# Adaptive FFN with Strassen-type products: transposing the maxima of the next x at the end of a step and scaling it ahead of the routing

## The chip, the cores and the metric

The kernel runs on one core of one Trainium2 chip. The metric is the device time of one execution in microseconds (us), here the median of three runs. A core has TensorE (PE), VectorE (DVE), ScalarE (ACT), GpSimd (POOL) and SyncE (SP), each with its own instruction stream that is executed in order; they wait for each other through semaphores. All DMAs of this kernel are issued from SP.

## The reference

```python
w = weights[subjects]                                # 32 items, 128 x 128 each
y = einsum('bct,bcd->bdt', x, w)                     # x: 32 x 128 x 2048, f32
result = einsum('bnd,od->bno', y, W_base) + b_base   # W_base: 2048 x 2048
probs = softmax(einsum('bnd,ed->bne', y, W_gate))    # 8 experts
top_p, top_i = top_k(probs, 2); top_p /= sum(top_p)
route_w = sum(one_hot(top_i, 8) * top_p[..., None])
h = einsum('bnd,erd->bner', y, A)                    # rank 16 for each expert
delta = einsum('bner,eor->bno', h * route_w, B)
out = x + result + delta
```

## The kernel before, in words

Items go in pairs, 16 pairs. The contraction over 2048 is cut in two halves, so there are `NSTEP` = 32 steps: steps 0 to 15 (`n < NP`) do the first half of the contraction for each pair and store partial rows, steps 16 to 31 (`second`) do the second half, the routing and the low-rank `delta`. All matmuls are f16, each operand split in an upper and a lower part (three matmuls for one product, `three`). A step multiplies two blocks (`s` = 0 and 1) by a seven-product scheme: `product(n, s, q)`, q = 0 to 6, 12 matmuls of 128x512 each. Below, q0 to q6 are the products with s = 0.

While step n multiplies, step n+1 is prepared. The prepared x must be scaled by powers of two, and that takes a chain over four engines:

- `find_maxima` (DVE, lines 659 and 661) reduces the loaded x and the item weights to `amax`, 128x4.
- `transpose_maxima` (PE, line 1067) transposes `amax` into `bank_c`; `find_top` (DVE, lines 666, 652, 653, 670) makes the four maxima into a diagonal `top_diag`, 4x4, bf16.
- `spread_maxima` (PE, line 1071) spreads it over all partitions; `scale_x` (DVE, lines 675 to 679) makes `xw_scale` and sums half of x.
- `split_x_hi` (ACT, lines 466, 467) and `split_x_lo` (DVE, lines 684, 686) split x and the weights, twice each, and `cond(n+1, ...)` (PE, three matmuls a column, into `bank_c`) multiplies them. `cond(n+1, U_A11)` stands behind q5, needs the first `split_x_lo`, and is followed by q6.

The other work of a step: `make_features` (48 small matmuls into `bank_h`, between q0 and q1) gives the routing features; `features` (DVE, 728, 736) scales them. In the second half `route_tokens` (DVE, 745 to 767) computes the routing in small linked operations; its softmax needs one exponential from ACT (line 606 before, 610 in the change), which line 761 waits for. `weigh_features` (DVE, 774 to 788) gives `hw`, `transpose_hw` stands behind q4 on PE, ACT takes the upper part of the transposed `hwT` (line 611) and DVE the lower (794). `finish` (DVE, 716 and 720) joins products into output tiles: C11, C12, C21, C22 for each block; POOL adds each to the output rows (line 429; in the first half also the bias, line 419). `copy_p` (ACT, line 506) copies products from PSUM: P1 (q0), P5 (q1), U2 (q3) and P4 (q4). The U2 copy overwrites what C11 reads, so it waits for C11.

The order on each engine is the order in which the code is written; no scheduler changes it. Before step 0, PE, ACT, DVE and POOL prepare the first half of W (`w_quads`, `w_upper`, `w_sums_and_lower`, `w_lower`), and between steps 15 and 16 the second.

Of the kernel before, what the change touches and what calls it, by code (L numbers as in the profile page):

```python
# [13 lines left out]
NSTEP = 2 * NP  # L14
# [38 lines left out]
def adaln_ffn_kernel(nc, x, idx, w_cond, w_base, b_base, w_gate, a_lora, b_lora, out):  # L53
# [4 lines left out]
    with ExitStack() as ctx:  # L58
# [206 lines left out]
        P1_COPY, P5_COPY, U2_COPY, P4_COPY = range(4)  # L265
# [194 lines left out]
        def _(act):  # L460
            def split_x_hi(n, i):
                if i == 0:
                    act.wait_ge(x_scaled, n + 1)
                else:
                    act.wait_ge(xs_added, n + 1)
                nc.scalar.activation(XP[:, 0, i, :], X[:, i, :], ACT.Copy, scale=xw_scale[:, i:i + 1])
                nc.scalar.activation(WCP[:, 0, i, :], WC[:, i, :], ACT.Copy,
                                     scale=xw_scale[:, 2 + i:3 + i]).then_inc(xp_hi, 1)
# [24 lines left out]
            def copy_p(n, s, i):  # L493
                par = n % 2
                src, q, at, row = ((BX[s], 0, 0, 0), (BY[1], 1, 1, 1), (BX[s], 3, 0, 0), (BZ, 4, 2, 1))[i]
                act.wait_ge(prod_done, n_prod(n, s, q))
                before = 2 * n + s - 1
                if i == P1_COPY and before >= 0:
                    act.wait_ge(t_done, n_tile(before // 2, before % 2, C12))
                elif i == U2_COPY:  # L500
                    act.wait_ge(t_done, n_tile(n, s, C11))
                elif i == P5_COPY and before >= 0:
                    act.wait_ge(t_done, n_tile(before // 2, before % 2, C22))
                elif i == P4_COPY and before >= 0:
                    act.wait_ge(t_done, n_tile(before // 2, before % 2, C21))
                nc.scalar.activation(PC[:, at, :], src[:, :], ACT.Copy,  # L506
                                     scale=y_inv[:, par, row:row + 1]).then_inc(p_copied, 1)
# [93 lines left out]
            for n in range(NSTEP):  # L601
                more = n + 1 < NSTEP
                copy_p(n, 0, P1_COPY)
                if n >= NP:
                    act.wait_ge(shifted_ready, n - NP + 1)
                    nc.scalar.activation(exps[:, :, :], shifted[:, :, :], ACT.Exp).then_inc(exps_ready, 1)
                copy_p(n, 0, P5_COPY)
                copy_p(n, 0, U2_COPY)
                if n >= NP:
                    act.wait_ge(hwT_filled, n - NP + 1)  # L610
                    nc.scalar.activation(hwT[:, 0, :], BD[:, 0:2 * P], ACT.Copy).then_inc(hwT_hi, 1)
                if more:
                    split_x_hi(n + 1, 0)
                    split_x_hi(n + 1, 1)
                copy_p(n, 0, P4_COPY)
                if more:
                    copy_a(n + 1, U_A11)
                    s_upper(n + 1, A11)
                    copy_a(n + 1, U_S1)
                    s_upper(n + 1, S1)  # L620
                copy_p(n, 1, P1_COPY)
                if more:
                    copy_a(n + 1, U_A12)
                    s_upper(n + 1, A12)
                    s_upper(n + 1, S2)
                copy_p(n, 1, P5_COPY)
                if more:
                    copy_a(n + 1, U_A22)
                    s_upper(n + 1, A22)
                    s_upper(n + 1, S4)  # L630
                    s_upper(n + 1, S3)
                copy_p(n, 1, U2_COPY)
                copy_p(n, 1, P4_COPY)
                if n == NP - 1:
                    sum_rows(NU)
                    for g in range(NU, 2 * NU):
                        if g + 1 < 2 * NU:
                            sum_rows(g + 1)
                        w_upper(g)
                    act.wait_ge(w_sum_lo, 4 * 2 * NU)  # L640

        @block.vector
        def _(dve):
# [283 lines left out]
            w_sums_and_lower(7)  # L927

            find_maxima(1)
            for n in range(NSTEP):  # L930
                more, second = n + 1 < NSTEP, n >= NP
                features(n)
                if more:
                    find_top(n + 1)
                if second:
                    route_tokens(n)
                    weigh_features(n)
                finish(n, 0, C11)
                if more:
                    scale_x(n + 1)  # L940
                if second:
                    split_hwT_lo(n)
                if more:
                    split_x_lo(n + 1, 0)
                    split_x_lo(n + 1, 1)
                finish(n, 0, C12)
                if second:
                    add_delta(n, 0)
                finish(n, 0, C21)
                finish(n, 0, C22)  # L950
                if second:
                    add_delta(n, 1)
                if more:
                    s_lower(n + 1, A11)
                    s_lower(n + 1, S1)
                if second:
                    add_delta(n, 2)
                if more:
                    sum_s2(n + 1)
                    s_lower(n + 1, A12)  # L960
                if second:
                    add_delta(n, 3)
                finish(n, 1, C11)
                if more:
                    s_lower(n + 1, S2)
                if second:
                    add_delta(n, 4)
                if more:
                    sum_s4_s3(n + 1)
                    s_lower(n + 1, A22)  # L970
                if second:
                    add_delta(n, 5)
                if more:
                    s_lower(n + 1, S4)
                    s_lower(n + 1, S3)
                if n + 2 < NSTEP:
                    find_maxima(n + 2)
                finish(n, 1, C12)
                if second:
                    add_delta(n, 6)  # L980
                    add_delta(n, 7)
                finish(n, 1, C21)
                finish(n, 1, C22)
                if n == NP - 1:
                    dve.wait_ge(r_added, 8 * NP)
                    w_scales(NU)
                    for g in range(NU, 2 * NU):
                        if g + 1 < 2 * NU:
                            w_scales(g + 1)
                        w_sums_and_lower(g)  # L990

        @block.tensor
        def _(pe):
# [158 lines left out]
            cond(0, U_A22)  # L1152
            w_quads(6)
            w_quads(7)

            for n in range(NSTEP):
                more, second = n + 1 < NSTEP, n >= NP
                if n in (0, NP):
                    prepared = NU * (1 + n // NP)
                    pe.wait_ge(w_lo, 3 * prepared)  # L1160
                    pe.wait_ge(w_sum_lo, 4 * prepared)
                    pe.wait_ge(w_inv, prepared)
                product(n, 0, 0)
                make_features(n)
                if more:
                    transpose_maxima(n + 1)
                for q in range(1, NPROD):
                    product(n, 0, q)
                    if q == 2 and more:
                        spread_maxima(n + 1)  # L1170
                    if q == 4 and second:
                        transpose_hw(n)
                    if q == 5 and more:
                        cond(n + 1, U_A11)
                    if q == 6:
                        if more:
                            cond(n + 1, U_S1)
                        if second:
                            delta(n, 0)
                for q in range(NPROD):  # L1180
                    product(n, 1, q)
                    if q < 2 and more:
                        cond(n + 1, (U_A12, U_A22)[q])
                    if second and q < 6:
                        delta(n, q + 1)
                        if q == 5:
                            delta(n, 7)
                if n == NP - 1:
                    pe.wait_ge(p_copied, n_copy(n, 1, P4_COPY))
                    pe.wait_ge(t_done, n_tile(n, 1, C22))  # L1190
                    pe.wait_ge(h_ready, NP)
                    for g in range(NU, 2 * NU):
                        pe.wait_ge(stage_in[2 * g % 4], 16 * (g // 2 + 1))
                        pe.wait_ge(stage_in[(2 * g + 1) % 4], 16 * (g // 2 + 1))
                        w_quads(g)
# [27 lines left out]
```

## Time and profile before

| What | Value |
|---|---|
| Median of 3 runs | 1655.74 us (1655.5 to 1656.36) |
| The profiled execution | 1655.53 us, its span 1653.7 us |
| PE busy | 1530.8 us (93%) |
| DVE busy | 1301.4 us (79%) |
| ACT busy | 595.5 us (36%) |
| POOL busy | 615.8 us (37%) |
| Granted TensorE clock, mean | 0.973 |

Busy time of an engine is the sum of its instructions' spans. In the timeline of this trace a matmul of 128x512 is shown 0.38 us long, though the next one starts some 0.215 us after it: the ends are modelled. So PE times are best taken from start to start.

### The profile page before, as it was taken

To read this page: it belongs to the slowest core of one execution; us is meant where nothing else is said; L and a number is where in the kernel's file an instruction comes from. 1 tells how busy PE (TensorE), PEld (TensorE's weight loads), DVE (VectorE), ACT (ScalarE), POOL (GpSimd) and SP (SyncE) were. 2 spreads that over 40 slices of the span, in tenths; PEclk is the share of its full clock that TensorE was granted. 3 is DMA by queue.
4 is the path that set the end of the run, shared out by engine and by line. 5 is a ranking of instruction groups with operands and counts; after the bars stand their busy time and mean duration, and the time that the engine had idled before them with its cause. 6 is when DMAs were issued, how large, how long until landed. Compare 5 with 4: busy or idle time off the path is not lost.

```text
span 1653.7 us, 25726 instructions
## 1 busy us (share of the span) xinstructions
PE 1530.8 (93%) x9539; PEld 832.7 (50%) x9539; DVE 1301.4 (79%) x2234; ACT 595.5 (36%) x996; POOL 615.8 (37%) x467
## 2 busy tenths in 40 slices
PE   5359999999999999999659999999999999999998
PEld 4245555555555555555454555545554554554553
DVE  4777888888888888888776888888888888888874
ACT  6563333333333333333583322333332233333231
POOL 2253555555555555555461212212221221221222
PEclk9679999999999999999889999999999999999999
DMA  5243444444444444444622334434324443332432
GB/s 193 87 143 90 134 134 134 135 135 132 134 133 132 128 135 134 135 135 137 212 89 79 93 99 134 133 98 129 111 82 121 134 119 111 122 102 84 135 106 70
DMA packets 102911, 201.87 MB, mean 122 GB/s; under 512 B 10874, under 2 KB 24186, under 8 KB 102266
## 3 DMA queue, kind: packets, MB, share of 16 engines
q1 hardware_dynamic: 102786, 200.22, 39.4%
q8 instruction: 76, 1.25, 0.3%
q14 instruction: 49, 0.40, 0.1%
HBM read 128.96 MB, written 71.22 MB: 121 GB/s over the span
## 4 chain that ended last, share of the span: by engine, by line
PE 76%; DVE 15%; ACT 4%; issue 4%; DMA 1%; POOL 1%; SPq 0%; POOLq 0%; ACTq 0%; DVEq 0%
PE bank_x L995 9%; PE bank_x L996 9%; PE bank_x L997 9%; PE bank_y L997 8%; PE bank_y L996 8%; PE bank_y L995 8%; PE bank_h L997 3%; PE bank_h L995 3%; PE bank_h L996 3%; PE bank_z L997 3%; PE bank_z L995 3%; PE bank_z L996 3%; PE bank_c L995 2%; PE bank_c L996 2%; PE bank_c L997 2%
## 5 line engine op out<-in xcount | busy, mean ns | idle before, releaser
L429 POOL TENSOR_TENSOR x_res<-x_res,t_sums 128x512 f32<-128x512 f32 x256 | 344.7, 1349 | 924.6 <-DVE t_sums L720 769.7
L995 PE MATMUL bank_x<-TT,s_parts 128*128 128x512 f16 x768 | 293.1, 382 | 13.3 <-POOL TT L413 7.5
L996 PE MATMUL bank_x<-TT,s_parts 128*128 128x512 f16 x768 | 292.8, 381 | 0.0
L997 PE MATMUL bank_x<-TT,s_parts 128*128 128x512 f16 x768 | 292.6, 381 | 0.0
L995 PE MATMUL bank_y<-TT,s_parts 128*128 128x512 f16 x768 | 291.1, 379 | 0.0
L996 PE MATMUL bank_y<-TT,s_parts 128*128 128x512 f16 x768 | 291.1, 379 | 0.0
L997 PE MATMUL bank_y<-TT,s_parts 128*128 128x512 f16 x768 | 291.1, 379 | 0.0
L506 ACT ACTIVATE p_copies<-bank_x,y_inv 128x512 f32<-128x512 f32 x128 | 87.4, 683 | 440.5 <-PE bank_x L997 346.6
L491 ACT ACTIVATE s_parts<-a_full 128x512 f16<-128x512 f32 x224 | 141.0, 630 | 270.6 <-DVE a_full L698 123.3
L720 DVE TENSOR_TENSOR t_sums<-t_sums,inv_w 128x512 f32<-128x512 f32 x256 | 218.7, 854 | 8.8
L419 POOL TENSOR_TENSOR x_res<-x_res,BT 128x512 f32<-128x512 f32 x128 | 199.3, 1557 | 1.2
L693 DVE TENSOR_TENSOR s_parts<-a_full,s_parts 128x512 f16<-128x512 f32 x224 | 192.0, 885 | 3.0 <-ACT s_parts L491 3.0
L716 DVE SCALAR_TENSOR_TENSOR t_sums<-bank_y,y_inv,p_copies 128x512 f32<-128x512 f32 x128 | 95.3, 745 | 78.2 <-PE bank_y L997 77.3
L995 PEld LDWEIGHTS bank_x<-TT,s_parts 128*128 128x128 f16 x768 | 75.3, 98 | 96.2 <-issue 15.3
L997 PEld LDWEIGHTS bank_x<-TT,s_parts 128*128 128x128 f16 x768 | 75.5, 98 | 91.8 <-issue 1.9
L997 PEld LDWEIGHTS bank_y<-TT,s_parts 128*128 128x128 f16 x768 | 75.2, 98 | 90.6
L716 DVE SCALAR_TENSOR_TENSOR t_sums<-bank_x,y_inv,p_copies 128x512 f32<-128x512 f32 x128 | 95.2, 744 | 30.7 <-PE bank_x L997 30.7
L996 PEld LDWEIGHTS bank_x<-TT,s_parts 128*128 128x128 f16 x768 | 75.4, 98 | 82.0 <-issue 1.4
L996 PEld LDWEIGHTS bank_y<-TT,s_parts 128*128 128x128 f16 x768 | 75.1, 98 | 81.7
L995 PEld LDWEIGHTS bank_y<-TT,s_parts 128*128 128x128 f16 x768 | 75.2, 98 | 81.2
L995 PE MATMUL bank_c<-w_cond_parts,x_parts 128*128 128x128 f16 x512 | 93.0, 220 | 23.7 <-DVE w_cond_parts L686 15.5
L474 ACT ACTIVATE a_full<-bank_c 128x512 f32<-128x512 f32 x128 | 76.1, 594 | 101.2 <-PE bank_c L997 101.2
(214 smaller groups left out, 2717.6 us busy)
## 6 DMA issues: line engine op xcount, KB each, us to landing
x<-in_x_dram SPq DMA_DIRECT2D x32, 1024.0 KB, 5.5
x_res<-in_x_dram SPq DMA_DIRECT2D x128, 256.0 KB, 3.7
part_scratch<-x_res SPq DMA_DIRECT2D x128, 256.0 KB, 3.0
x_res<-part_scratch SPq DMA_DIRECT2D x128, 256.0 KB, 4.0
out_dram<-x_res SPq DMA_DIRECT2D x128, 256.0 KB, 3.0
x_res<-in_L_ffn_W_base_dram SPq DMA_DIRECT2D x12, 512.0 KB, 4.6
w_cond<-in_L_cond_weights_dram SPq DMA_DIRECT2D x64, 64.0 KB, 3.9
a_full<-in_L_ffn_W_base_dram SPq DMA_DIRECT2D x8, 512.0 KB, 4.7
```

The lines of the kernel that those rows point to most:

```text
L419: link(nc.gpsimd.tensor_tensor(XR[:, xr_slot(m), :], XR[:, xr_slot(m), :], bias[:, o:o + Q], ALU.add))
L429: nc.gpsimd.tensor_tensor(XR[:, xr_slot(m), :], XR[:, xr_slot(m), :], TM[:, m % 2, :], ALU.add).then_inc(r_added, 1)
L474: nc.scalar.activation(AF[:, u, :], BC[:, :], ACT.Copy, scale=Y_DOWN).then_inc(af_copied, 1)
L491: nc.scalar.activation(SO[:, slot(n, q), 0, :, :], quads(AF[:, af_of[q], :]), ACT.Copy).then_inc(s_hi, 1)
L506: nc.scalar.activation(PC[:, at, :], src[:, :], ACT.Copy, scale=y_inv[:, par, row:row + 1]).then_inc(p_copied, 1)
L693: nc.vector.tensor_tensor(SO[:, slot(n, q), 1, :, :], quads(AF[:, af_of[q], :]), SO[:, slot(n, q), 0, :, :], ALU.subtract).then_inc(s_lo, 1)
L716: nc.vector.scalar_tensor_tensor(out=TM[:, m % 2, :], in0=src[:, :], scalar=y_inv[:, n % 2, c // 2:c // 2 + 1], in1=PC[:, at, :], op0=ALU. ...
L720: nc.vector.tensor_tensor(TM[:, m % 2, :], TM[:, m % 2, :], inv_w[:, o:o + Q], ALU.mult).then_inc(r_ready, 1)
L995: nc.tensor.matmul(dst, lhs[0], rhs[0], start=start, stop=False, skip_group_check=chained)
L996: nc.tensor.matmul(dst, lhs[0], rhs[1], start=False, stop=False, skip_group_check=chained)
L997: return nc.tensor.matmul(dst, lhs[1], rhs[0], start=False, stop=stop, skip_group_check=chained)
```

## The change

`transpose_maxima(n + 2)` now stands at the end of step n on PE, behind the last product, and the one for step 1 in front of step 0. `spread_maxima(n + 1)` stands right behind `make_features(n)`, where it was between q2 and q3. On DVE, `find_top(n + 2)` stands at the end of step n, and `scale_x(n + 1)` right behind `features(n)`, in front of the routing and of C11. On ACT the P5 copy and both `split_x_hi` stand in front of the exponential. The number of instructions on each engine is the same, and on SP and POOL nothing moves.

```diff
@@ ScalarE, the loop over the steps
                 copy_p(n, 0, P1_COPY)
+                copy_p(n, 0, P5_COPY)
+                if more:
+                    split_x_hi(n + 1, 0)
+                    split_x_hi(n + 1, 1)
                 if n >= NP:
                     act.wait_ge(shifted_ready, n - NP + 1)
                     nc.scalar.activation(exps[:, :, :], shifted[:, :, :], ACT.Exp).then_inc(exps_ready, 1)
-                copy_p(n, 0, P5_COPY)
                 copy_p(n, 0, U2_COPY)
                 if n >= NP:
                     act.wait_ge(hwT_filled, n - NP + 1)
                     nc.scalar.activation(hwT[:, 0, :], BD[:, 0:2 * P], ACT.Copy).then_inc(hwT_hi, 1)
-                if more:
-                    split_x_hi(n + 1, 0)
-                    split_x_hi(n + 1, 1)
                 copy_p(n, 0, P4_COPY)
@@ VectorE
             find_maxima(1)
+            find_top(1)
             for n in range(NSTEP):
                 more, second = n + 1 < NSTEP, n >= NP
                 features(n)
                 if more:
-                    find_top(n + 1)
+                    scale_x(n + 1)
                 if second:
                     route_tokens(n)
                     weigh_features(n)
                 finish(n, 0, C11)
-                if more:
-                    scale_x(n + 1)
                 if second:
                     split_hwT_lo(n)
@@
                 finish(n, 1, C21)
                 finish(n, 1, C22)
+                if n + 2 < NSTEP:
+                    find_top(n + 2)
@@ TensorE
             w_quads(7)
+            transpose_maxima(1)
@@
                 make_features(n)
                 if more:
-                    transpose_maxima(n + 1)
+                    spread_maxima(n + 1)
                 for q in range(1, NPROD):
                     product(n, 0, q)
-                    if q == 2 and more:
-                        spread_maxima(n + 1)
@@
                         if q == 5:
                             delta(n, 7)
+                if n + 2 < NSTEP:
+                    transpose_maxima(n + 2)
```

TensorE in front of step 0, before. The matmuls of line 1021 are the last of the preparation of W, the first of line 995 belongs to `product(0, 0, 0)`:

```order
L1004 MATMUL bank_h<-diag_inv,ones 128x128 x2
L1021 MATMUL bank_y<-diag,BT 128x128 x4
L1021 MATMUL bank_z<-diag,x_res 128x128 x4
L1021 MATMUL bank_x<-diag,BT 128x128 x4
L1021 MATMUL bank_x<-diag,x_res 128x128 x4
L995 MATMUL bank_x<-TT,s_parts 128x512
```

The same place in the change (its lines are one higher here):

```order
L1005 MATMUL bank_h<-diag_inv,ones 128x128 x2
L1022 MATMUL bank_y<-diag,BT 128x128 x4
L1022 MATMUL bank_z<-diag,x_res 128x128 x4
L1022 MATMUL bank_x<-diag,BT 128x128 x4
L1022 MATMUL bank_x<-diag,x_res 128x128 x4
L1068 MATMUL bank_c<-ident,amax 4x128
L996 MATMUL bank_x<-TT,s_parts 128x512
```

The transpose of the maxima of step 1 now stands in front of the first product.

ScalarE in a step of the second half, from the P1 copy, before (`p_copies` from `bank_x` is P1 and then U2, from `bank_y` P5, from `bank_z` P4):

```order
L506 ACTIVATE p_copies<-bank_x,y_inv 128x512
L606 ACTIVATE exps<-shifted 128x16
L506 ACTIVATE p_copies<-bank_y,y_inv 128x512
L506 ACTIVATE p_copies<-bank_x,y_inv 128x512
L611 ACTIVATE hwT<-bank_d 128x256
L466 ACTIVATE x_parts<-x,xw_scale 128x1024
L467 ACTIVATE w_cond_parts<-w_cond,xw_scale 128x128
L466 ACTIVATE x_parts<-x,xw_scale 128x1024
L467 ACTIVATE w_cond_parts<-w_cond,xw_scale 128x128
L506 ACTIVATE p_copies<-bank_z,y_inv 128x512
```

The same place in the change:

```order
L506 ACTIVATE p_copies<-bank_x,y_inv 128x512
L506 ACTIVATE p_copies<-bank_y,y_inv 128x512
L466 ACTIVATE x_parts<-x,xw_scale 128x1024
L467 ACTIVATE w_cond_parts<-w_cond,xw_scale 128x128
L466 ACTIVATE x_parts<-x,xw_scale 128x1024
L467 ACTIVATE w_cond_parts<-w_cond,xw_scale 128x128
L610 ACTIVATE exps<-shifted 128x16
L506 ACTIVATE p_copies<-bank_x,y_inv 128x512
L614 ACTIVATE hwT<-bank_d 128x256
L506 ACTIVATE p_copies<-bank_z,y_inv 128x512
```

The exponential moved behind the P5 copy and the four operations that split x.

VectorE from the end of one step of the second half into the next, the difference:

```order
+L666 TENSOR_REDUCE amax_top<-bank_c 4x1
+L652 TENSOR_SCALAR top_clamped<-amax_top 4x1
+L653 TENSOR_SCALAR top_pow<-top_clamped 4x1
+L670 TENSOR_SCALAR top_diag<-ident,top_pow 4x4
 L728 SCALAR_TENSOR_TENSOR h<-bank_h,y_inv,inv_ag 128x136 x2
 L736 TENSOR_TENSOR h<-h,h_first 128x272
-L666 TENSOR_REDUCE amax_top<-bank_c 4x1
-L652 TENSOR_SCALAR top_clamped<-amax_top 4x1
-L653 TENSOR_SCALAR top_pow<-top_clamped 4x1
-L670 TENSOR_SCALAR top_diag<-ident,top_pow 4x4
+L675 COPY pow<-bank_c 128x4
+L676 RECIPROCAL rpow<-pow 128x4
```

The four operations of `find_top` moved in front of the features, right behind C22 of the step before, and `scale_x` follows the features.

## Rows read from the trace of the kernel before

**Rows 1.** Timeline in front of step 0: start us, us, engine, line, op, out<-in, shapes, xcount

```profile
119.00 0.59 PE L995 MATMUL bank_x<-TT,s_parts 128*128 128x512 f16 x1 [7.45 <-POOL TT L413]
...
121.66 2.29 DVE L659 TENSOR_REDUCE amax<-x 128x2 f32<-128x2048 f32 x1 [4.52 <-DMA x<-in_x_dram]
123.86 0.41 DVE L661 TENSOR_REDUCE amax<-w_cond 128x2 f32<-128x256 f32 x1
```

**Rows 2.** Timeline of TensorE, step 23 (second half); in brackets idle us and its releaser

```profile
1217.07 0.27 PE L1067 MATMUL bank_c<-ident,amax 128*4 128x128 f32 x1
1217.18 0.38 PE L995 MATMUL bank_y<-TT,s_parts 128*128 128x512 f16 x1
...
1222.14 0.38 PE L997 MATMUL bank_y<-TT,s_parts 128*128 128x512 f16 x1
1222.45 0.17 PE L1071 MATMUL bank_c<-top_diag,ones 4*128 4x4 bf16 x1
1222.56 0.39 PE L995 MATMUL bank_x<-TT,s_parts 128*128 128x512 f16 x1
...
1231.74 0.23 PE L995 MATMUL bank_c<-w_cond_parts,x_parts 128*128 128x128 f16 x1 [1.02 <-DVE w_cond_parts L686]
```

**Rows 3.** Timeline of VectorE, end of step 22 and step 23

```profile
1214.92 1.27 DVE L720 TENSOR_TENSOR t_sums<-t_sums,inv_w 128x512 f32<-128x512 f32 x1
...
1218.41 0.28 DVE L666 TENSOR_REDUCE amax_top<-bank_c 4x1 f32<-4x128 f32 x1
...
1219.07 0.22 DVE L670 TENSOR_SCALAR top_diag<-ident,top_pow 4x4 bf16<-4x4 f32 x1
...
1221.68 0.17 DVE L761 TENSOR_REDUCE exp_sum<-exps 128x2 f32<-128x16 f32 x1
...
1225.37 0.42 DVE L788 SCALAR_TENSOR_TENSOR hw<-hw,hw_rpow 128x256 f32<-128x256 f32 x1
...
1226.49 0.69 DVE L720 TENSOR_TENSOR t_sums<-t_sums,inv_w 128x512 f32<-128x512 f32 x1
...
1230.13 1.28 DVE L684 SCALAR_TENSOR_TENSOR x_parts<-x,xw_scale,x_parts 128x1024 f16<-128x1024 f32 x1 [0.39 <-ACT w_cond_parts L467]
1231.34 0.35 DVE L686 SCALAR_TENSOR_TENSOR w_cond_parts<-w_cond,xw_scale,w_cond_parts 128x128 f16<-128x128 f32 x1
```

**Rows 4.** Timeline of GpSimd: adding C21 and C22 of step 22, C11 of step 23

```profile
1214.37 1.27 POOL L429 TENSOR_TENSOR x_res<-x_res,t_sums 128x512 f32<-128x512 f32 x1 [1.44 <-DVE t_sums L720]
1216.34 1.27 POOL L429 TENSOR_TENSOR x_res<-x_res,t_sums 128x512 f32<-128x512 f32 x1 [0.69 <-DVE t_sums L720]
1227.33 1.27 POOL L429 TENSOR_TENSOR x_res<-x_res,t_sums 128x512 f32<-128x512 f32 x1 [9.73 <-DVE t_sums L720]
```

**Rows 5.** Timeline of the preparation of W: `find_top(0)` beside GpSimd

```profile
71.03 1.17 DVE L670 TENSOR_SCALAR top_diag<-ident,top_pow 4x4 bf16<-4x4 f32 x1
...
71.03 1.15 POOL L413 TENSOR_TENSOR TT<-t_sums,TT 128x512 f16<-128x512 f32 x1
```

**Rows 6.** Timeline of ScalarE, step 23

```profile
1219.60 0.22 ACT L606 ACTIVATE exps<-shifted 128x16 f32<-128x16 f32 x1 [4.49 <-DVE shifted L746]
1219.97 0.69 ACT L506 ACTIVATE p_copies<-bank_y,y_inv 128x512 f32<-128x512 f32 x1
...
1226.55 0.69 ACT L506 ACTIVATE p_copies<-bank_x,y_inv 128x512 f32<-128x512 f32 x1 [5.89 <-DVE t_sums L716]
1228.17 0.38 ACT L611 ACTIVATE hwT<-bank_d 128x256 f16<-128x256 f32 x1 [0.93 <-PE bank_d L1095]
1228.66 1.15 ACT L466 ACTIVATE x_parts<-x,xw_scale 128x1024 f16<-128x1024 f32 x1
```

**Rows 7.** Timeline of VectorE, GpSimd and TensorE where a first-half step begins

```profile
251.84 0.99 DVE L720 TENSOR_TENSOR t_sums<-t_sums,inv_w 128x512 f32<-128x512 f32 x1
...
252.35 1.60 POOL L429 TENSOR_TENSOR x_res<-x_res,t_sums 128x512 f32<-128x512 f32 x1
...
253.63 0.27 PE L1067 MATMUL bank_c<-ident,amax 128*4 128x128 f32 x1
```

## The prediction

> **What bounds the kernel now.** I first read the page: TensorE is busy 93% of the span at a mean clock of 0.973, so it sets the pace, and what counts is where it idles. Then the list of waits of TensorE, then the timeline of one step of each half, all engines side by side. In the steps of the first half TensorE runs product after product and never waits. In steps 16 to 30 it waits once a step: cond(n+1, U_A11), behind q5, starts at 1231.74 after 1.02 us of idleness, released by split_x_lo on VectorE [rows 2, 3]. Because the modelled end of the matmul ahead of it lies 0.17 us past the point at which a next one could start (0.38 shown, 0.215 from start to start), the whole loss is 1.19 us a step, 15 times. That is all the change can win: 17.9 us.
>
> What VectorE did in that time is a chain: features, find_top, routing, hw, C11, scale_x, then the split on ScalarE and VectorE. The change takes find_top and scale_x off its end. So I follow the new chain, with TensorE's first matmul of q1 (1217.18 before) as its zero. Before, cond starts 14.56 us after it [rows 2].
>
> **The start.** PE runs in order, and transpose_maxima(1) now stands in front of the first product. It needs find_maxima(1), whose x lands late: VectorE waited 4.52 us for that DMA and ended line 661 at 124.27. TensorE had begun step 0 at 119.00 [rows 1]. In the change its first product can start at 124.27, plus 0.05 for the semaphore (line 686 ends at 1231.69, cond starts at 1231.74 [rows 2, 3]), plus 0.11 for the transpose: 124.4, **5.4 us later**. Before, a whole product of the step covered this reduction. Nothing behind it has slack for it, since the first half is TensorE's. The shown 0.59 us of the matmul at 119.00, against 0.38 in step 23, says that TensorE restarts at its lower clock after the idle time [rows 1, 2]; it does so after a longer idle time too, so I add nothing, and bound the term by 3 and 8 us.
>
> **The transpose and the spread, as such.** The transpose costs 0.11 us on TensorE (1217.07 to 1217.18) wherever it stands. The spread between q2 and q3 cost 0.21: the last matmul of q2 starts at 1222.14, the spread at 1222.45, q3 at 1222.56, 0.42 where 0.21 is usual [rows 2]. Behind the features it costs 0.11 as long as it needn't wait.
>
> **It will wait.** top_diag is made by the last operation of find_top, line 670, now directly behind C22. In step 22, C22's line 720 ends at 1216.19, line 670 would start 0.58 later (line 666 starts 0.08 before the end of its predecessor, line 670 0.66 after line 666) at 1216.77. But GpSimd's add of C22 runs from 1216.34 to 1217.61 [rows 3, 4]. Do the two disturb each other? The one time that line 670 met a GpSimd add, it took 1.17 us instead of 0.22 and ended 0.02 us after that add [rows 3, 5]. Hence it ends at 1217.63, and the spread starts at 1217.68. TensorE comes to it at 1217.18 (1217.07, and 0.11 later because the transpose is now in front of q0): it idles 0.50 us. q1 starts at 1217.79 instead of 1217.18, **+0.61 a step**, against TensorE's other work; 0.21 of it is saved again at q3.
>
> In the first half: line 720 ends at 252.83, line 670 would start at 253.41, GpSimd's add lasts to 253.95, so line 670 ends at 253.97, the spread starts at 254.02, q1 at 254.13. Before it started 0.11 behind the transpose, at 253.74 [rows 7]. +0.39, less the 0.21 saved: **+0.18 a step**, for steps 1 to 15 (find_top(1) and find_top(17) have time enough): 2.7 us. The rest of a first-half step stays under TensorE's cover: the splits now come earlier, and cond did not wait before. If line 670 were not held, the spread wouldn't wait: 0.11 less 0.21, -0.10 a step.
>
> **The new chain of a second-half step**, from the start of q1. The P5 copy follows the end of q1: 1219.97 less 1217.18, at 2.79 [rows 2, 6]. It blocks ScalarE some 0.6 (0.69 shown, the next starts 0.1 earlier). The scale has long been there, so both split_x_hi follow: one pair takes from 1228.66 to just before 1230.13, 1.43, two with their overlaps 2.7 [rows 3, 6]. Only then comes the exponential, 0.22 [rows 6]: VectorE can start line 761 at 6.31 (2.79 + 0.58 + 2.68 + 0.22 + 0.04). Is it VectorE that is late? From the end of line 670 at 1217.63 it has the features (1.2, from the end of TensorE's features some 0.15 after 1217.07 to line 666 at 1218.41), scale_x (at most 2.6: from 1227.18 to 1230.13 less 0.39 idle, and it met an add of GpSimd's there) and the routing up to line 761 (2.39, from 1219.29 to 1221.68) [rows 3]. It is ready at 1223.8 or sooner, 6.0 after q1 at most: ScalarE decides, and VectorE waits for the exponential, which before was there in time. Behind the exponential everything is queued on VectorE: line 788 starts 3.69 later, C11 behind it.
>
> From line 761: hw at 3.69; the U2 copy, which waits for C11, at 4.87 (1226.55 less 1225.37); hwT on ScalarE at 5.45, its end at 5.83; the lower part of hwT on VectorE (shaped as line 788, 0.42) from 5.87; split_x_lo could start at 6.20. GpSimd's add of C11 starts at 5.65 (1227.33 less 1225.37, plus 3.69) and ends at 6.92 [rows 3, 4, 6]. Line 684 reads two tensors in SBUF, as line 720 does, and line 720 took 1.27 us instead of 0.69 when the add of C21 at 1214.37 had begun before it, going on about 0.14 before that add's end at 1215.64 [rows 3, 4]. So line 684 is taken up at 6.78, and cond starts 1.61 after it (1231.74 less 1230.13), at 8.39. With 6.31 that is 14.70 after q1.
>
> That line 684 itself is held is in no row: it never met an add before, and took 1.28 us, as in step 23. The page "SBUF — State Buffer" of the Trainium skill, section "Who interferes with whom", says that a VectorE instruction with two SBUF inputs contends with a GpSimd instruction that reads SBUF and that the later one is blocked to the end. By that rule cond starts at 14.70; were the page wrong for this instruction, 14.12. The trace agrees for line 720, 1.27 against 0.69 [rows 3].
>
> A step of the second half changes by 14.70 - 14.56 = +0.14 in the chain and +0.61 in the start of q1: **+0.75 us**, for steps 17 to 30, 10.5 us; step 16 has only the +0.14. transpose_hw waits 0.1 or so on the way (line 788 ends 4.11 after 761, at 10.4; TensorE is there at 10.3), which is hidden in front of cond. So the wait for split_x_lo does not go: it stands behind the exponential instead of behind scale_x.
>
> **Sum.** 5.4 + 2.7 + 0.1 + 10.5 = 18.7. The profiled execution took 1655.53 us (span 1653.7, and 1.8 around it), the median is 0.2 above it: 1674.4 us.
>
> **Rivals.**
> - *The splits are not held by GpSimd's add.* Then the chain is 8.39 less 0.58 long, cond at 14.12: 0.44 less in step 16, +0.17 in 14 steps. 5.4 + 2.7 - 0.4 + 2.4 = 10.1: 1665.8 us. For it: that no row shows line 684 held; against it: line 720. Chance 0.15.
> - *Line 670 is not held at the end of a step.* q1 starts 0.5 sooner in the second half and 0.28 in the first. 5.4 - 1.5 + 0.1 + 14 x 0.25 = 7.5: 1663.2 us. Against it stands the one case that there is [rows 5]. Chance 0.08. Both together: 5.4 - 1.5 - 0.4 - 14 x 0.33 = -1.1, 1654.6 us, within what can be told from no change; chance 0.04.
> - *Faster: the exponential is not on the path, cond finds its input ready.* Then a step has +0.40 at q3 and -1.19 at cond: 14 times -0.79, step 16 -1.4, with 5.4 + 2.7: -4.4, 1651.4 us. For it: x's split now stands early on ScalarE. Its point: cond could start 13.2 after q1 (14.56 less 1.19 and 0.21), so the exponential would have to come 1.5 us sooner than 6.31. It would without the two splits in front of it. Chance 0.07.
> - *More than that:* the idle time at the start costs more clock, or the collisions with GpSimd, whose adds now meet more of VectorE's work, spread on: 1680 us, chance 0.08.
> - The forecast itself has 0.58.
>
> **How the numbers follow.** The range goes from under the first two rivals (1662) to 1679; outside are the rivals below and part of the last. A measurement of this kernel tells some 0.2%, 3.3 us, from no change. Faster by more than that: 0.07. Within it: 0.05. Slower: 0.88.
>
> **What the profile of the changed kernel would show.** Step 0's first matmul at some 124.4. Line 670 with about 0.55 us in the first half and 0.86 in the second. TensorE waiting for top_diag at the spread, 0.3 us in 15 steps and 0.5 in 14. VectorE idle in front of line 761 for the exponential, 0.3 us or more. The lower split's first operation near 1.9 us in the second half, and TensorE still waiting for line 686 in 15 steps, 1.0 us and more by the modelled ends. A second-half step 0.75 us longer than before, a first-half step 0.18. I am wrong if line 761 finds the exponential ready, or if the first product of step 0 starts as before.

## The result, and the profile after

| What | Before | Changed |
|---|---|---|
| Median of 5 runs | 1655.74 us (1654.92 to 1656.44) | 1674.44 us (1672.8 to 1674.85) |
| Ratio | | 1.0111, 95% interval 1.0098 to 1.0123 |
| The profiled execution | 1655.53 us, span 1653.7 | 1674.5 us, span 1672.7 |

The change costs 18.7 us. The page of the changed kernel, its part on busy time:

```profile
PE 1537.3 (92%) x9539; PEld 834.4 (50%) x9539; DVE 1324.4 (79%) x2234; ACT 592.5 (35%) x996; POOL 630.4 (38%) x467
```

The work of TensorE is the same and its share is smaller: the time went into waits. VectorE and GpSimd are busy 23 and 15 us longer with the same number of instructions: an operation that one of them is made to wait in by the other (it is *held*) shows as a longer one. On VectorE line 684 is busy 23.3 us longer in all, line 686 15.8 and line 670 14.4. Line 677 (`xw_scale`, 128x4) is busy 27.1 us less: before, it was held too, in 31 of 32 steps. In step 23:

```profile
1227.50 1.12 DVE L677 TENSOR_SCALAR xw_scale<-rpow 128x4 f32<-128x4 f32 x1
```

before, ending 0.02 us after GpSimd's add of C11 [rows 4], and in the change:

```profile
1232.55 0.17 DVE L677 TENSOR_SCALAR xw_scale<-rpow 128x4 f32<-128x4 f32 x1
```

The split of x on ScalarE started 0.04 us after the held one ended [rows 6], so this hold was part of the chain that made cond late before. No kernel removes it alone.

The list of waits, TensorE's and the one of VectorE that matters (who waited, for whom, us in total, times, longest us):

```profile
PE bank_c L996 <- DVE w_cond_parts L686: 16.7, 15, 1.1
PE bank_c L1072 <- DVE top_diag L670: 14.6, 15, 9.9
PE bank_c L1068 <- DVE amax L661: 12.5, 1, 12.5
...
DVE exp_sum L761 <- ACT exps L610: 26.3, 15, 2.1
```

The wait for the lower split (line 686) that the change might have removed is still there, 15 times. Two are new: TensorE for `top_diag` (9.9 of the 14.6 us is one wait in the preparation, which the kernel before has too; the other 14 are 0.34 us each, in the second half), and once for the maxima. VectorE's wait for the exponential is new too.

The timeline of VectorE, GpSimd, ScalarE and TensorE where step 23 begins; it answers to [rows 2 to 4] and [rows 6]. The columns are as there:

```profile
1230.26 0.85 DVE L670 TENSOR_SCALAR top_diag<-ident,top_pow 4x4 bf16<-4x4 f32 x1
...
1237.62 0.17 DVE L761 TENSOR_REDUCE exp_sum<-exps 128x2 f32<-128x16 f32 x1 [1.75 <-ACT exps L610]
...
1243.49 0.42 DVE L794 SCALAR_TENSOR_TENSOR hwT<-bank_d,hwT 128x256 f16<-128x256 f32 x1 [0.36 <-ACT hwT L614]
1243.83 1.78 DVE L684 SCALAR_TENSOR_TENSOR x_parts<-x,xw_scale,x_parts 128x1024 f16<-128x1024 f32 x1
```

```profile
1229.82 1.26 POOL L429 TENSOR_TENSOR x_res<-x_res,t_sums 128x512 f32<-128x512 f32 x1 [0.70 <-DVE t_sums L720]
1243.27 1.26 POOL L429 TENSOR_TENSOR x_res<-x_res,t_sums 128x512 f32<-128x512 f32 x1 [12.18 <-DVE t_sums L720]
```

```profile
1234.07 0.69 ACT L506 ACTIVATE p_copies<-bank_y,y_inv 128x512 f32<-128x512 f32 x1 [5.36 <-PE bank_y L998]
1234.65 1.14 ACT L466 ACTIVATE x_parts<-x,xw_scale 128x1024 f16<-128x1024 f32 x1
...
1237.32 0.20 ACT L610 ACTIVATE exps<-shifted 128x16 f32<-128x16 f32 x1
```

```profile
1231.16 0.17 PE L1072 MATMUL bank_c<-top_diag,ones 4*128 4x4 bf16 x1 [0.34 <-DVE top_diag L670]
1231.27 0.39 PE L996 MATMUL bank_y<-TT,s_parts 128*128 128x512 f16 x1
...
1245.93 0.23 PE L996 MATMUL bank_c<-w_cond_parts,x_parts 128*128 128x128 f16 x1 [1.12 <-DVE w_cond_parts L686]
```

Read from above: line 670 begins 0.44 us after GpSimd's add and ends 0.03 us after it. 0.05 us later TensorE spreads, and q1 starts at 1231.27. The exponential starts 6.05 us after q1, behind P5 and both splits; VectorE had stood 1.75 us before it came. GpSimd's add of C11 begins at 1243.27; the first lower split comes up at 1243.83, takes 1.78 us and ends 1.08 us after that add. cond starts 14.66 us after q1, against 14.56 before.

The timeline in front of step 0 and at a first-half step, as [rows 1] and [rows 7]:

```profile
121.12 2.29 DVE L659 TENSOR_REDUCE amax<-x 128x2 f32<-128x2048 f32 x1 [4.23 <-DMA x<-in_x_dram]
123.33 0.41 DVE L661 TENSOR_REDUCE amax<-w_cond 128x2 f32<-128x256 f32 x1
...
257.79 0.56 DVE L670 TENSOR_SCALAR top_diag<-ident,top_pow 4x4 bf16<-4x4 f32 x1
```

```profile
256.74 1.59 POOL L429 TENSOR_TENSOR x_res<-x_res,t_sums 128x512 f32<-128x512 f32 x1
```

```profile
123.79 0.37 PE L1068 MATMUL bank_c<-ident,amax 128*4 128x128 f32 x1 [12.50 <-DVE amax L661]
124.00 0.59 PE L996 MATMUL bank_x<-TT,s_parts 128*128 128x512 f16 x1
...
258.41 0.17 PE L1072 MATMUL bank_c<-top_diag,ones 4*128 4x4 bf16 x1
```

The first product starts at 124.00, 5.0 us later than in [rows 1], because the transpose in front of it waits for an x that lands late. In the first-half step line 670 ends 0.02 us after GpSimd's add, and the spread follows it by 0.06.

To see where the 19 us of span (1672.7 against 1653.7) went, take the first matmul of `make_features` in steps 1, 15, 16 and 31; from one step's to the next one's is a period. Timeline of the changed kernel:

```profile
170.69 0.22 PE L996 MATMUL bank_h<-FT,s_parts 128*128 128x136 f16 x1
...
762.79 0.22 PE L996 MATMUL bank_h<-FT,s_parts 128*128 128x136 f16 x1
...
881.68 0.32 PE L996 MATMUL bank_h<-FT,s_parts 128*128 128x136 f16 x1
...
1622.91 0.22 PE L996 MATMUL bank_h<-FT,s_parts 128*128 128x136 f16 x1
```

and of the kernel before:

```profile
166.59 0.22 PE L995 MATMUL bank_h<-FT,s_parts 128*128 128x136 f16 x1
...
755.99 0.22 PE L995 MATMUL bank_h<-FT,s_parts 128*128 128x136 f16 x1
...
873.36 0.22 PE L995 MATMUL bank_h<-FT,s_parts 128*128 128x136 f16 x1
...
1603.93 0.22 PE L995 MATMUL bank_h<-FT,s_parts 128*128 128x136 f16 x1
```

| Stretch | Before | Changed | More | Forecast |
|---|---|---|---|---|
| Up to step 1 | 166.59 | 170.69 | 4.10 | 5.4 |
| Steps 1 to 15, 14 periods | 589.40 | 592.10 | 2.70 (0.19 each) | 2.5 |
| Step 15 to 16, with the second half of W | 117.37 | 118.89 | 1.52 | 0.2 |
| Steps 16 to 31, 15 periods | 730.57 | 741.23 | 10.66 | 10.6 |

### The profile page after: what moved, and what is told of

It is laid out like the page before. It is cut to its first block, busy times and chain, and to the rows that moved or that the text cites. A ratio compares the mean times of both kernels' runs of the same rounds, so it can differ in the third digit from the quotient of the medians.

```text
span 1672.7 us, 25710 instructions
## 1 busy us (share of the span) xinstructions
PE 1537.3 (92%) x9539; PEld 834.4 (50%) x9539; DVE 1324.4 (79%) x2234; ACT 592.5 (35%) x996; POOL 630.4 (38%) x467
## 4 chain that ended last, share of the span: by engine, by line
PE 62%; DVE 23%; ACT 7%; issue 5%; DMA 1%; POOL 0%; SPq 0%; DVEq 0%; POOLq 0%; ACTq 0%
PE bank_y L996 8%; PE bank_x L996 8%; PE bank_x L998 8%; PE bank_x L997 8%; PE bank_y L998 8%; PE bank_y L997 8%; DVE t_sums L716 3%; DVE amax L659 2%; DVE t_sums L720 2%; ACT x_parts L466 2%; PE bank_c L996 2%; PE bank_z L998 2%; PE bank_z L996 2%; PE bank_z L997 2%; PE bank_c L998 2%
## 5 line engine op out<-in xcount | busy, mean ns | idle before, releaser
L429 POOL TENSOR_TENSOR x_res<-x_res,t_sums 128x512 f32<-128x512 f32 x256 | 359.1, 1405 | 928.7 <-DVE t_sums L720 773.7
```

Source lines behind the costliest of these rows:

```text
L429: nc.gpsimd.tensor_tensor(XR[:, xr_slot(m), :], XR[:, xr_slot(m), :], TM[:, m % 2, :], ALU.add).then_inc(r_added, 1)
```

## The experiments

All ran beside the kernel before, whose median in the three series was 1655.42, 1655.33 and 1655.53 us. The change is at 1674.44, from the series in which the kernel before had 1655.74. A timeline is that of one execution. The executions of one kernel lie 1.2 to 2.8 us apart, so medians that differ by less than some 1.5 us are not told apart here.

**Step 0 in the old order.** In step 0 alone TensorE and VectorE keep the order of before:

```diff
             w_quads(7)
-            transpose_maxima(1)
...
                 make_features(n)
-                if more:
+                if n == 0:
+                    transpose_maxima(1)
+                elif more:
                     spread_maxima(n + 1)
                 for q in range(1, NPROD):
                     product(n, 0, q)
+                    if q == 2 and n == 0:
+                        spread_maxima(1)
...
                 features(n)
-                if more:
+                if n == 0:
+                    find_top(1)
+                elif more:
                     scale_x(n + 1)
```

(and `scale_x(1)` behind C11, `find_top(1)` no longer in front of the loop).

> The changed kernel, with step 0 alone in the order of before: transpose_maxima(1) behind make_features(0), its spread behind q2, find_top(1) and scale_x(1) at their old places on VectorE. Steps 1 to 31 as in the change. Theory (TensorE's first product stands behind the transpose and so behind the late x): the first product starts near 119 again and the whole comes 4 to 5 us sooner than the change, some 1670 us. Rival (the late start is absorbed later, or the clock takes it back): within 1 us of 1674.4.

Measured: 1667.64 us (1667.31 to 1668.64), ratio 1.0075 (1.0061 to 1.0088), 6.8 us under the change. The first product starts at 118.69 and `make_features` of step 1 at 165.83, 4.9 us sooner than in the change, and that stays to step 15. A further 1.4 us falls between steps 15 and 16 and 0.6 behind step 16, where both programs are the same; more on that below. The theory holds, the rival falls.

**The exponential first.** ScalarE in the order P1, exponential, P5, splits; all else as in the change:

```diff
                 copy_p(n, 0, P1_COPY)
+                if n >= NP:
+                    act.wait_ge(shifted_ready, n - NP + 1)
+                    nc.scalar.activation(exps[:, :, :], shifted[:, :, :], ACT.Exp).then_inc(exps_ready, 1)
                 copy_p(n, 0, P5_COPY)
                 if more:
                     split_x_hi(n + 1, 0)
                     split_x_hi(n + 1, 1)
-                if n >= NP:
-                    act.wait_ge(shifted_ready, n - NP + 1)
-                    nc.scalar.activation(exps[:, :, :], shifted[:, :, :], ACT.Exp).then_inc(exps_ready, 1)
```

> The changed kernel, with the exponential on ScalarE back in front of the P5 copy and of the splits of x. Theory (the exponential behind P5 and four split operations is what makes VectorE's chain late): line 761 no longer waits 1.75 us for the exponential, it starts some 4.6 us after q1 instead of 6.35, and cond comes at 13.1 to 13.3 after q1 instead of 14.66, practically without a wait: 15 x 1.4 to 1.5, 1652 to 1654 us. Rival (another link holds cond, such as hwT on ScalarE or GpSimd's add before the split): the wait shrinks by less than half, 1664 us or more.

Measured: 1651.66 us (1650.42 to 1652.43), ratio 0.9976 (0.9967 to 0.9986): 22.8 us under the change, and under the kernel before. Its timeline where step 23 begins, VectorE, GpSimd and TensorE:

```profile
1224.36 0.17 DVE L761 TENSOR_REDUCE exp_sum<-exps 128x2 f32<-128x16 f32 x1
...
1230.93 0.42 DVE L794 SCALAR_TENSOR_TENSOR hwT<-bank_d,hwT 128x256 f16<-128x256 f32 x1 [1.07 <-ACT hwT L614]
1231.27 1.28 DVE L684 SCALAR_TENSOR_TENSOR x_parts<-x,xw_scale,x_parts 128x1024 f16<-128x1024 f32 x1
```

```profile
1230.00 1.27 POOL L429 TENSOR_TENSOR x_res<-x_res,t_sums 128x512 f32<-128x512 f32 x1 [10.46 <-DVE t_sums L720]
```

```profile
1219.62 0.17 PE L1072 MATMUL bank_c<-top_diag,ones 4*128 4x4 bf16 x1 [0.34 <-DVE top_diag L670]
1219.72 0.39 PE L996 MATMUL bank_y<-TT,s_parts 128*128 128x512 f16 x1
...
1232.90 0.22 PE L996 MATMUL bank_c<-w_cond_parts,x_parts 128*128 128x128 f16 x1
```

Line 761 starts 4.64 us after q1 with no idle time in brackets, cond 13.18 after q1 and without a wait. The split now comes up as GpSimd's add ends, so it is not held either: 1.28 us. So the 1.48 us that cond gains on q1 have two parts: the collision, which the lateness caused and which is worth 0.5 by the kernel further down that removes it alone, and the lateness itself.

**The exponential behind P5.** As above, but with P5 left in front of it:

```diff
                 copy_p(n, 0, P1_COPY)
                 copy_p(n, 0, P5_COPY)
+                if n >= NP:
+                    act.wait_ge(shifted_ready, n - NP + 1)
+                    nc.scalar.activation(exps[:, :, :], shifted[:, :, :], ACT.Exp).then_inc(exps_ready, 1)
                 if more:
                     split_x_hi(n + 1, 0)
                     split_x_hi(n + 1, 1)
```

(the exponential behind the splits goes).

> The changed kernel with the exponential between the P5 copy and the splits of x. Of what stands in front of it in the change only the splits (2.7 us) go, the P5 copy (from the end of q1 on) stays. The exponential would come some 3.4 us after q1, VectorE is ready for it at 4.6: nothing is lost against having it first, 1651 to 1652.5 us. Rival (P5, which waits for q1, is a good part of the delay): 1656 us or more.

Measured: 1650.78 us (1649.98 to 1651.71), ratio 0.9972 (0.9962 to 0.9983). The exponential starts 3.38 us after q1, and line 761 at 4.64 as above. P5 in front of the exponential costs nothing; the four split operations cost it all.

**The diagonal by ScalarE.** `find_top(n)` ends with `top_pow2` for n > 0, and ScalarE, idle at the end of a step, makes `top_diag`:

```diff
+            def make_diag(n):
+                act.wait_ge(top_ready, n)
+                act.wait_ge(amax_spread, n)
+                nc.scalar.activation(top_diag[:, :], ident[0:4, 0:4], ACT.Copy,
+                                     scale=top_pow2[:, 0:1]).then_inc(amax_top_ready, 1)
...
                 copy_p(n, 1, U2_COPY)
                 copy_p(n, 1, P4_COPY)
+                if n + 2 < NSTEP:
+                    make_diag(n + 2)
```

> The changed kernel, with top_diag of steps 1 to 31 made by ScalarE instead of VectorE's line 670, at the same place in the program; same values. Theory (line 670 is held by GpSimd's add of C22 and holds the spread): ScalarE is not held, the spread no longer waits, 0.28 us less in each of 15 first-half steps and 0.5 in each of 14 second-half steps: 11 us, 1663 us. Rival (the spread is late because find_top as such comes too late behind C22, and the 1.2 GHz hand-over costs as much): 1671 us or more.

Measured: 1665.68 us (1664.4 to 1667.05), ratio 1.006 (1.0047 to 1.0074), 8.8 us under the change. TensorE's timeline at a spread of the second half has no idle time any more, and the hand-over through ScalarE is in time:

```profile
1225.36 0.22 PE L1013 MATMUL bank_h<-FT,s_parts 128*128 128x136 f16 x1
1225.51 0.17 PE L1087 MATMUL bank_c<-top_diag,ones 4*128 4x4 bf16 x1
1225.62 0.39 PE L1011 MATMUL bank_y<-TT,s_parts 128*128 128x512 f16 x1
```

```profile
1225.01 0.30 ACT L465 ACTIVATE top_diag<-ident,top_pow 4x4 bf16<-4x4 f32 x1 [9.74 <-DVE top_pow L681]
```

A first-half period is back at 42.10 us (42.29 in the change, 42.10 before), a second-half one goes from 49.40 to 49.00. So the hold of line 670 is shown as the cause of the wait at the spread. I had expected 11 us, from 0.28 and 0.5 us a step; the steps gained 0.19 and 0.4. The rows say why: from the last matmul of the features to q1 it is 0.26 us even without a wait, where 0.06 is the usual distance of those matmuls. The spread behind the features costs 0.20 us, about the 0.21 that it cost between q2 and q3, and not 0.11. The kernel with neither transpose nor spread behind the features (the last one below) says the same: from the first matmul of the features to q1 it takes 2.84 us, here 3.04.

**GpSimd's add of C11 behind the split.**

```diff
+                if n >= NP and j == 0 and n + 1 < NSTEP:
+                    pool.wait_ge(xp_lo, 2 * (n + 1) + 1)
                 pool.wait_ge(r_ready, m + 1)
```

> The changed kernel, with GpSimd's add of C11 in steps 16 to 30 waiting for the first lower split of x. Theory (line 684 is held by that add): line 684 takes 1.28 instead of 1.78 us, cond comes 0.5 us sooner in 15 steps, 7.5 us, 1667 us. Rival (line 684 is slow for another reason, or the add that comes later holds what follows): 1672 us or more.

Measured: 1665.71 us (1665.09 to 1667.05), ratio 1.0061 (1.0048 to 1.0075), 8.7 us under the change. VectorE's split and GpSimd's add in step 23:

```profile
1240.14 1.27 DVE L686 SCALAR_TENSOR_TENSOR x_parts<-x,xw_scale,x_parts 128x1024 f16<-128x1024 f32 x1
...
1241.59 1.28 DVE L686 SCALAR_TENSOR_TENSOR x_parts<-x,xw_scale,x_parts 128x1024 f16<-128x1024 f32 x1
```

```profile
1241.81 2.19 POOL L431 TENSOR_TENSOR x_res<-x_res,t_sums 128x512 f32<-128x512 f32 x1 [14.41 <-DVE w_cond_parts L688]
```

The split takes 1.27 instead of 1.78 us, and now it is the add that is held by the second split, 2.19 instead of 1.26, which costs TensorE nothing that shows. The period of a second-half step is 48.89 instead of 49.40. cond still waits, but starts 14.15 us after q1 (1227.58) instead of 14.66:

```profile
1241.73 0.23 PE L998 MATMUL bank_c<-w_cond_parts,x_parts 128*128 128x128 f16 x1 [0.60 <-DVE w_cond_parts L688]
```

**Both holds away, the exponential still late.** The last two edits together.

> The changed kernel with both meetings with GpSimd removed (top_diag by ScalarE, GpSimd's add of C11 behind the first lower split), the exponential left behind the splits. If the two holds are separate costs, 8.8 and 8.7 us come off: 1656 to 1658 us, so that what is left over the kernel before is the late x at the start. Rival (they overlap, since both act on the same chain): 1661 us or more.

Measured: 1658.81 us (1657.65 to 1660.21), ratio 1.0019 (1.001 to 1.0029), 15.6 us under the change where the two alone gave 8.8 and 8.7; I had expected 1656 to 1658. In the steps they add: a first-half step takes 42.10 us and a second-half step 48.48, 0.92 less than in the change where the two alone gave 0.40 and 0.51. In the profiled execution (the slowest of 11, 1660.21 us) step 1 comes 5.8 us later than before and the stretch between steps 15 and 16 takes 2.2 us more; the steps of the second half are 0.21 us each under those of the kernel before. So the 3.3 us over the kernel before are the start and the middle, less what the second half saves.

**Putting the useful parts together.** Four more kernels look for what of the change is worth having. The first joins the old order of step 0 and the early exponential:

> Both mendings together: the exponential back in front of the P5 copy, and step 0 in the order of before. The two costs lie in different steps, so they should add: 22.8 and some 5 to 6.8 us under the change, 1645 to 1647 us. Rival (one hides part of the other): 1650 us.

Measured: 1645.64 us (1644.87 to 1646.24), ratio 0.994 (0.9926 to 0.9954), 28.8 us under the change where the two alone gave 6.8 and 22.8. They nearly add.

The next has `make_diag` as well:

> As c1, and top_diag of steps 1 to 31 by ScalarE, so that nothing behind C22 is held by GpSimd. If the hold of line 670 is a cost of its own, 15 x 0.2 and 14 x 0.5 us come off again: 1636 to 1638 us, and TensorE waits neither at the spread nor at cond. Rival (with the exponential early, GpSimd's add of C11 becomes the bound of cond, since it starts with VectorE's chain): only the first half gains, 1643 us.

Measured: 1638.92 us (1638.26 to 1639.47), ratio 0.9901 (0.9886 to 0.9916). TensorE's waits for line 686 and for `top_diag` in the loop are both gone; this version is faster than the kernel before by 1.0% and than the change by 2.1%. That is 1 us over the 1636 to 1638 expected: a second-half step takes 47.55 us against 47.90, and the stretch between steps 15 and 16 took 118.51 us in the profiled execution against 117.64 in the version without `make_diag`.

The third keeps the change's step 0 and has x of step 1 loaded sooner:

```diff
             sp.wait_ge(w_tr, 4 * (NU - 1))
+            sp.wait_ge(xp_lo, 2)
+            load_x(1)
             for m in range(4):
                 load_tile(m)
```

> The changed kernel with the exponential first and top_diag by ScalarE, step 0 as in the change, but SyncE issues the load of step 1's x in front of the first tiles of x_res and the bias. If the late x alone is what held the first product, it starts within 1.5 us of 119 with the transpose still in front of it: within 2 us of c2. Rival (the transfers of W and the bias then come late instead): 2 us or more above c2.

Measured: 1641.23 us (1640.38 to 1642.12), ratio 0.9916 (0.9902 to 0.9929). The first product starts at 119.73, though the transpose is still in front of it: the late x alone made it late. The total is 2.3 us above the version with the old step 0, which is where I had put the rival (2 us or more). The steps do not differ (42.10 us, and 47.54 against 47.55). Of the 2.1 us between the two profiled executions, 0.4 is the later start (119.29 there), 1.0 the product q0 of step 0 (5.01 us at a granted clock of 0.51, 4.00 at 0.64 there) and 0.9 the stretch between steps 15 and 16. Whether the earlier load has a part in the last two is not shown.

The last takes one part of the change only, the transpose and `find_top` at the end of a step, with the spread, `scale_x` and ScalarE as before:

```diff
                 finish(n, 1, C21)
                 finish(n, 1, C22)
+                if n + 2 < NSTEP:
+                    find_top(n + 2)
```

> The kernel of before with one part of the change: the maxima are transposed and find_top done at the end of a step (in step 0 at their old places). The spread stays behind q2, scale_x behind C11, ScalarE as before. Theory: find_top's 0.8 us leave VectorE's chain in front of the routing, of which the hold of line 670 gives back 0.3; TensorE meets no wait at the spread, cond comes 0.5 us sooner in 15 steps, 7 to 8 us, 1648 us. Rival (GpSimd's add of C11 or of C22 takes it back, as in the change): 1654 us or more.

Measured: 1651.62 us (1651.18 to 1652.85), ratio 0.9978 (0.9969 to 0.9987), a gain of 3.7 us, half of what I expected. The timeline of ScalarE in step 23 says why:

```profile
1226.40 0.39 ACT L611 ACTIVATE hwT<-bank_d 128x256 f16<-128x256 f32 x1 [1.46 <-PE bank_d L1097]
1226.68 1.14 ACT L466 ACTIVATE x_parts<-x,xw_scale 128x1024 f16<-128x1024 f32 x1
```

VectorE's chain is 0.5 us shorter (line 761 starts 3.98 us after q1 against 4.50, rows 2 and 3), but the splits stand on ScalarE behind the upper part of hwT, and that waits for a transpose behind q4 on TensorE, 10.99 us after q1 as before. So the split starts at 11.27 against 11.48, and a second-half step takes 48.47 us against 48.69: ScalarE's queue took 0.3 of the 0.5 us.

## Why the prediction was right

Its forecast, 1674.4 us, was met at 1674.44, and the sum is right in its two large places for the reasons given. That it fits to 0.1 us is luck: terms missed in opposite ways, and the start and the middle differ by more than that from one execution to the next.

- **The start, 5.4 us forecast.** The mechanism holds, with the old step 0 and with the early x. The first product started 5.0 us late, x having landed 0.5 us sooner in this execution; by step 1 it was 4.1. TensorE's product q0 took 4.59 us at a granted clock of 0.56, before 5.07 at 0.50 (the lower level, 1.2 GHz, all through). In this execution the term was 1.3 us too large. In the profiled executions of the five other kernels with the late x in front of the first product, step 1 began 4.35 to 5.76 us later than before, so 5.4 was a fair size and 4.1 a low draw.
- **The spread waits, 0.18 a step in the first half.** 0.19 measured. Line 670 took 0.56 us there and 0.85 in the second half, where 0.55 and 0.86 were forecast. The rival that line 670 is not held falls. But the prediction priced the spread behind the features at 0.11 us where it costs 0.20, and so counted a step without the wait 0.10 under the kernel before; with the diagonal made by ScalarE it is level with it, 42.10 us. As long as the spread waits, this error drops out of the sum, because the wait ends when line 670 does; it makes the rivals in which line 670 is not held too fast, by 0.1 us a step.
- **The chain of a second-half step, 14.70 after q1.** 14.66 measured, and q1 0.61 later as forecast: 0.71 a step (10.66 in all) where 0.75 in 14 steps and 0.14 in one were forecast. That one, step 16, took 0.68 more and not 0.14: some 0.35 is the lower clock, at which its features began (3.40 us from their first matmul to q1, 3.05 in the kernel with the old step 0), and 0.2 the transpose at its end and the dearer spread, which the sum left out there. Each link is in the profile: P5 at 2.80, the exponential at 6.05, line 761 at 6.35, cond 8.31 behind it. VectorE was ready for the exponential at 4.60, well before the 6.0 that the prediction gave as its bound.
- **The exponential decides.** Shown by both kernels that move it. The rival in which cond finds its input ready was put to the test: it is what the kernel becomes when the splits stand behind the exponential, with cond 13.18 after q1, the 13.2 given as its point, and a step 0.79 us under the one before (47.90 against 48.69), the -0.79 given.
- **The split is held by GpSimd's add.** This was in no row of before and rested on line 720's example and on the page "SBUF — State Buffer" of the Trainium skill, section "Who interferes with whom", whose rule on two SBUF inputs was weighed there. By that rule, the trace agrees: 1.78 us instead of 1.28, and 1.27 when the add stays away, with cond at 14.15 where the prediction had 14.12 for a split that is not held. Its sign "near 1.9 us" was 0.1 too large, with the split ending 1.08 us after the add.
- **A sign that came out smaller.** TensorE's waits for `top_diag` show in the 14 steps of the second half alone, at 0.34 us; 0.3 in 15 steps and 0.5 in 14 were forecast. The ends of matmuls are modelled, so this list shows less than the start of q1 does, which came as late as forecast.
- **What the sum did not have.** 1.5 us between steps 15 and 16, where 0.2 was forecast. The changed kernel's q0 of step 16 took 5.07 us at a granted clock of 0.50, before 4.21 at 0.61 (from its first matmul to the features), which is 0.9 of it. Six kernels, the change among them, have the same program in this stretch. Two took 118.9 us (the change, and the one with the later add of C11; q0 at 0.50 in both), four 117.1 to 117.6 (the exponential first, behind P5, the old step 0, and the two mendings together; q0 at 0.63 to 0.65), and the kernel before 117.4. So it is not caused by an instruction that the change moves there, and as each kernel has one profile it may be no more than the difference between two executions; what tips it was not tested.

The forecast "1654.6, within no change" for the case that neither hold occurs can be set beside the kernel that removes both, 1658.81: 4.2 us off. The steps explain some 3 of them, 0.10 in each of the first half (42.10, not 42.00) and 0.12 in each of the second (0.21 under the kernel before, not 0.33), most of it the price of the spread; the rest lies in the start and the middle.

## What to carry to other kernels

An operation moved to the front of an in-order queue is paid for by what it overtakes: here four idle-looking operations on an engine that is busy 36% delayed one exponential of 0.2 us, on which 4 us of another engine's work and the very input they were to hurry were waiting. Before you move a link of a chain, list what else passes through each queue it goes to, and check what the other user of a shared resource does at the new time; small operations fit an idle gap only if nobody holds them in it. A preload hoisted in front of a loop needs its data by then: look at the first iteration separately.

## What the runs showed of the hardware

- A VectorE operation on 4x4 elements (line 670, f32 in, bf16 out) is held for the rest of a GpSimd add like a large one: 0.85 and 0.56 us instead of 0.22, in every step whose C22 is being added beside it, ending 0.02 to 0.03 us after the add. So is line 677 (128x4, f32), 1.12 instead of 0.17 us in the kernel before. Lines 652 and 653, on 4x1 elements, ran beside the same add in 0.14 us each. The same diagonal made by ScalarE beside the same add took 0.30 us and was not held.
- The holder is whoever comes first: the first lower split, 1.78 instead of 1.28 us behind GpSimd's add; the add, 2.19 instead of 1.26 us behind the second split. In the changed kernel's first half one split of each step was held too (2.28 us), under cover of TensorE's products.
- The length of TensorE's first product q0 does not follow the idle time in front of it. Behind more than 12 us it took 3.84 to 5.07 us in six kernels (granted clock 0.67 to 0.50), behind 7.4 to 8.2 us 4.00 to 5.07 in six others (0.64 to 0.50).
- A matmul of 4x4 (bf16, 4 columns) in a stream of f16 matmuls costs TensorE 0.20 to 0.21 us from start to start, behind one of 128x512 as behind one of 128x136; the f32 transpose to 4 partitions costs 0.11 us.
